# A graph network on one Trainium2 core: wider fills between gathers, 16-bit places, and one gathered tile per chunk moved to TensorE

## What is computed

```
L0  messages = h[src] * edge_weight ; summed at dst
L1  messages = silu(einsum(h[dst], edge_attr_8, W)) @ W_lin ; summed at src
L2  msg = einsum('ei,eio->eo', h[src], W_rel[edge_type]) * e ; summed at dst      (90 relations)
L3  w = kernel_net(edge_attr_6)  (a 16x16 matrix for each edge)
    four times: msg = einsum('ei,eio->eo', nodes[src], w) ; mean at dst ; gelu
```

## Time and profile before

| what | value |
|---|---|
| time, median of 3 runs | 28610.86 us (28602.41 to 28721.83) |
| the profiled execution's own time | 28730.07 us |
| its span | 28728.3 us |
| busy share of the span | PE 78%, PEld 43%, DVE 61%, ACT 49%, POOL 75% |
| granted TensorE clock, mean | 0.864 of full speed |
| DMA | 3120.14 MB, mean 109 GB/s |

### The profile page before, as it was taken

How to read it: one execution, slowest core, us unless ns; L and a number is a source line. 1 busy time by engine, 2 the same in 40 slices (tenths; PEclk the granted TensorE clock), 3 DMA queues, 4 the chain that set the end, 5 groups by cost and what they waited for, 6 DMA issues and landing times. The chain is left out here.

```text
span 28728.3 us, 413713 instructions
## 1 busy us (share of the span) xinstructions
PE 22502.9 (78%) x109882; PEld 12362.4 (43%) x109882; DVE 17590.5 (61%) x29340; ACT 14192.2 (49%) x24676; POOL 21497.8 (75%) x31473
## 2 busy tenths in 40 slices
PE   7888668888878888867777777688886888778886
PEld 3444345555545555533434344333333333333333
DVE  5555468888867667744444444566665666656665
ACT  6666511111135444533333333477775777667775
POOL 7888878888867667766667677677777777777777
PEclk9999879999988888877778787799898889888898
DMA  3211235555532222222222222455554555555554
GB/s 98 45 45 44 46 74 92 94 92 94 92 68 66 64 64 65 66 62 87 90 88 94 87 91 92 125 173 173 174 172 142 172 172 174 158 156 171 172 172 138
DMA packets 2201230, 3120.14 MB, mean 109 GB/s; under 512 B 782486, under 2 KB 1548644, under 8 KB 2199460
## 3 DMA queue, kind: packets, MB, share of 16 engines
q1 hardware_dynamic: 1340898, 2927.73, 31.3%
q0 software_dynamic: 790944, 162.36, 8.3%
q10 hardware_dynamic: 69282, 28.92, 0.4%
HBM read 2443.85 MB, written 673.47 MB: 109 GB/s over the span
## 5 line engine op out<-in xcount | busy, mean ns | idle before, releaser
L772 POOL DMA_INDIRECT got<-table,idx x14310 | 14075.9, 984 | 6055.7 <-issue 3081.4
L790 PE MATMUL in_place<-place_hot,tparts 128*128 128x512 fp8e4 (+1 forms) x49950 | 12106.4, 399 | 2647.8 <-ACT place_hot L995 1563.8
L995 ACT ACTIVATE place_hot<-place_b,far_lanes 128x512 fp8e4<-128x512 f32 (+1 forms) x17550 | 10586.2, 683 | 8.8 <-PE in_place L790 8.8
L790 PEld LDWEIGHTS in_place<-place_hot,tparts 128*128 128x128 bf16 x49950 | 5100.3, 105 | 9003.7 <-issue 4843.7
L1599 POOL DMA_INDIRECT added<-rows,add_idx x2160 | 3602.4, 1668 | 714.3 <-issue 654.5
L968 ACT ACTIVATE mask<-contw 128x208 f32 (+2 forms) x1350 | 555.9, 412 | 5970.6 <-DVE run L1129 2705.2
L775 POOL MEMSET rest<- 128x128 f32 (+2 forms) x14310 | 3199.8, 224 | 10.2
L1216 DVE TENSOR_TENSOR prod<-wcopy,got 128x1024 f32<-128x1024 f32 x810 | 991.5, 1227 | 2990.9 <-ACT wcopy L947 1895.6
L1642 PE MATMUL acc<-hot,spread 128*128 128x392 bf16 x12960 | 2545.4, 350 | 0.0
L1107 DVE SCALAR_TENSOR_TENSOR picked<-range_b,range_col,in_place 128x512 f32<-128x512 f16 (+1 forms) x1350 | 962.7, 713 | 2553.8 <-DMA added<-rows,add_idx 2404.6
L1171 DVE TENSOR_TENSOR prod<-w_in,rows_p 128x2048 f32<-128x2048 f32 x810 | 1846.8, 2280 | 444.7 <-ACT rows_p L983 283.7
(11 more groups left out here) (250 smaller groups left out, 21896.4 us busy)
## 6 DMA issues: line engine op xcount, KB each, us to landing
w_in<-kept SPq DMA_DIRECT2D x2430, 512.0 KB
kept<-wcopy SPq DMA_DIRECT2D x810, 512.0 KB
place_b<-place_row SPq DMA_DIRECT2D x1080, 256.0 KB
got<-table,idx POOLq DMA_INDIRECT x14310
attr<-in_edge_attr SPq DMA_DIRECT2D x270, 768.0 KB
range_b<-range_row SPq DMA_DIRECT2D x1080, 128.0 KB
rows<-in_src_row SPq DMA_DIRECT2D x270, 512.0 KB
sums<-outb SPq DMA_DIRECT2D x1350, 96.0 KB
```

Of the source, the lines that this page charges most:

```text
L772: pool.indirect_dma_start(out=got[:, r, j * W:(j + 1) * W], out_offset=None, in_=table, in_offset=bass.IndirectOffsetOnAxis(ap=idx[:, r, j ...
L790: mm = pe.matmul(in_place[b][:, h, :], tparts[:, s, t, :], place_hot[:, b, t, h * XC:(h + 1) * XC], start=(t == 0 and s == 0), stop=(t == ...
L995: ins = act.activation(place_hot[:, b, t, :], place_b[:, b, :], ACT.Abs_reciprocal_sqrt, bias=SB["far_lanes"][:, t:t + 1], scale=HOT_SLOPE ...
```

## The change

Fills are 256 columns in every pass of `edge_pass`. In the relational pass X is 4 instead of 3, so TensorE fetches four tiles of a chunk and GpSimd gathers eight instead of nine. The places are 16-bit in DRAM and in SBUF: they are stored as whole numbers, and the shift that was added to them moves into the per-partition bias of the activations (`const_far_lanes`).

```diff
+RW = 256
-        place_row = dram("place_row", (EP + 2 * CE,))
+        place_row = dram("place_row", (EP + 2 * CE,), F16)
-        range16 = sb("range16", [P, T], F16)
+        range16, place16 = sb("range16", [P, T], F16), sb("place16", [P, T], F16)
-                for row, v in ((SB["place_row"], key), (SB["range_row"], range16)):
+                for row, v in ((SB["place_row"], place16), (SB["range_row"], range16)):
-                c.step(dve.tensor_scalar(key[:, :], key[:, :], PLACE_SHIFT, None, ALU.add))
+                c.step(dve.tensor_copy(place16[:, :], key[:, :]))
-    X = {"weighted": 4, "relational": C // 4, "kernel_net": 0, "kernel_kept": 4}[kind]
+    X = {"weighted": 4, "relational": 4, "kernel_net": 0, "kernel_kept": 4}[kind]
-        rest = sb("rest", [P, {"weighted": 256, "relational": 128, "kernel_net": 32, "kernel_kept": 128}[kind] * J0])
+        rest = sb("rest", [P, J0 * RW])
-        RW = rest.shape[1] // J0
-            place_b = sb("place_b", [P, HALVES, XE])
+            place_b = sb("place_b", [P, HALVES, XE], F16)
-        "const_far_lanes": -lanes() * np.float32(HOT_SLOPE),
+        "const_far_lanes": (PLACE_SHIFT - lanes()) * np.float32(HOT_SLOPE),
```

## The result

The changed kernel takes **27,584 us** (median of 4 runs, 27,545 to 27,588) against 28,661 (4 runs, 28,602 to 28,722) for the kernel before: a ratio of 0.962, 95% interval 0.959 to 0.965, so 3.8% faster.

What follows compares the result with a forecast made beforehand. It took GpSimd to bound the weighted pass, and TensorE with its loop, slowed by holes, the relational pass. Relational -620, net -200 and kept +80 made -740, so 27,870 us; 8-in-10 range 27,600 to 29,250.

Steps and rivals of the forecast that it cites:

- The reading: Relational, net and kept passes: closely spaced GpSimd gathers go with holes in TensorE's stream, or in net long unexplained chunks.
- the tile taken from it gives nothing by itself: Relational pass: GpSimd wasn't the bound, so one gather fewer gains nothing by itself.
- the 14 that the prediction names for nine tiles: Relational pass: with nine gathered tiles and the wide fill, GpSimd would need 14 us a chunk.
- The first rival: TensorE, relational pass: holes don't come from the gathers and stay, its added work costs 675 us; 29,370 us, chance 0.27.
- Relational, -620 forecast: Relational pass: holes go, a chunk falls from 15.6 to 13.3 us, times 270 chunks is 620 us less.
- The 12.7 us of TensorE work: Relational pass: TensorE's need per chunk at full clock with four tiles, 3.9 + 8.0 + 0.8 us.
- some 0.6 of waiting for ScalarE: Relational pass: TensorE waits some 0.6 us a chunk for ScalarE's one-hot blocks, added to its 12.7 us.
- Net, -200 forecast: Net pass: gain of 200 us, taken between a gain of 367 and a loss of 635.
- The floor: Net pass: GpSimd's work with wide fills, 5075 us or 18.8 a chunk, allows a gain of at most 367 us.
- Kept, +80 forecast: Three kept passes: wider fills charged 0.1 us a chunk for uneven chunks, 80 us; bounds 0 and 252 us a pass.
- The range: Whole kernel: 27,600 to 28,200 us if the case is right, 27,600 to 29,250 for 8 in 10.
- The second rival: GpSimd becomes the bound before the gain arrives: about 28,560 us, within 0.5% of the kernel before, chance 0.13.

Runs made afterwards that it cites:

- The runs on chips 7 and 2: Chip 7: changed kernel with other fill widths or fills behind the last gather, 28,459 to 28,585 us; chip 2: five kept tiles, wide fills 26,956, narrow 28,809.
- x3_tile_only: Kernel before with only the relational pass's ninth tile moved to TensorE (four instead of three), chip 13: 28,693 us against 29,218, ratio 0.982.
- e4_places_only: Kernel before with only the places made 16-bit, chip 11: 26,340 us against 26,329, ratio 1.0004.
- e3_tile_only: Kernel before with only four instead of three relational tiles on TensorE, chip 11: 26,277 us against 26,329, ratio 0.998.
- x2_fills_only: Kernel before with only the fills made 256 columns in all passes, chip 7: 27,802 us against 29,376, ratio 0.946.
- e1_old_widths: Changed kernel with the fill widths of before (256, 128, 32, 128 columns), chip 11: 26,279 us against 26,329 for the kernel before, ratio 0.998.

## Why the prediction was right, and where it wasn't

**The reading was right.** The forecast rested on four passes in which closer gathers and holes went together, and called that a coincidence. The runs on chips 7 and 2 make it a cause, on chips that show holes at all, though not the only one. The prediction also says of the ninth tile that "the tile taken from it gives nothing by itself". That step is wrong: x3_tile_only gives 525 us, with net and kept as they were. The wide fills alone leave the relational pass at 13.9 us a chunk, the 14 that the prediction names for nine tiles. The first rival (the holes come from elsewhere: 29,370) fell. The Trainium skill's rule beside it (SBUF — State Buffer, Who interferes with whom), that a DMA never contends with a compute engine, doesn't cover what was measured: 103 waits became 855 in the weighted pass with narrower fills between the gathers, and the load of places halved.

**The sum was too small; what failed is the size of three terms.**
- *Relational, -620 forecast, -741 measured.* The 12.7 us of TensorE work were exact. The step that failed is "some 0.6 of waiting for ScalarE". It was taken over from a quick chunk with three tiles, where TensorE came to the blocks early. With four tiles TensorE has 2.2 us more of its own to do, and ScalarE only 1.4, so the wait closes: 5.9 us in the whole pass. On chip 11, without holes, it is seen by itself: 96.6 us with three tiles (e4_places_only), 1.2 with four (e3_tile_only), both with 128 columns and in the same stretch. Measured are 12.85 us a chunk, not 13.3; 0.45 x 270 is the 121 us.
- *Net, -200 forecast, -384 measured.* The floor was right (18.8 us a chunk, 367 to gain). The step that failed is taking a value between no gain and the floor, where only the closeness of the gathers was weighed and nothing spoke for a partial gain: if the spacing is the cause, the widest fill removes all holes and GpSimd's work is what is left.
- *Kept, +80 forecast, -51 measured.* The 80 were charged for uneven chunks, and the lower bound was 0. The step that failed is that charge: the passes came out a little shorter, not longer, with 24 holes for 332. The bound "nothing" excluded a gain without a reason; the spread of single chunks had grown narrower instead (8.5 to 16.9 us between the 5th and 95th percentile before, 9.9 to 13.6 after).

The three differences (121, 184, 131) with the weighted pass's 10 are 446 against the profiled executions (-1,185 for -740). The medians fell by 1,077, less than the two profiles did: the profiled execution before was slower than all its kernel's other ones, the one after the fastest of its four. The forecast also stood on a median of 28,611, which a fourth run made 28,661. So the miss of 286 us looks better than the sum was, by chance.

**The range** ended at 27,600 because it kept the relational term at its point value and kept at zero. With the relational pass at TensorE's bare 12.7 us (-780 instead of -620) its low end would have been 27,440. The 20 us that the low end also takes off are worked out from nothing in the text. The floors of three passes were all worked out there; a low end that takes them together would have held the result.

**The second rival** (GpSimd becomes the bound first) was half true: GpSimd is the bound in net and kept now, but what it costs is less than what the holes had cost. On chip 11 there are none, and it is the outcome there.

**What was not foreseen** is that the sign depends on the chip. The profile of one chip can't show it.

## What to carry to other kernels

If TensorE stands still for 0.2 to 1 us at "issue" in some passes and not in others, compare how far apart the indirect DMAs of GpSimd are issued; a filler instruction between them, not behind them, may pay, and only as wide as the engine's slack allows. When such a step removes a disturbance, take the pass's next bound as the estimate, not a point halfway, and let the range's low end be the sum of those bounds. Time such a change on several chips: here one kernel took 26,329 us on one chip and 29,376 on another, and the wide fills alone are worth 5.4% on the one with 29,376 and cost 5.7% on the other.

## What the runs showed of the hardware

- The same program took 26,329 to 29,376 us from chip to chip (11.6%), within 0.6% on each. Four numbered chips lie at 29,218 or above, one at 26,329, the first chip at 28,661. The passes with widely spaced gathers agree everywhere (weighted 12.3 to 12.4 us a chunk, scatter 15.8), those with close gathers don't (net 16.6 to 20.8, kept 11.4 to 12.7).
- In the relational pass of the kernel before the median hole is 0.46 us, and eight in ten lie between 0.24 and 0.98. What resource is disturbed isn't settled: the trace names none. TensorE isn't the only one that suffers. The 79 common standstills of net on the first chip are 76 on chip 15 with the kernel before, and none with wide fills (the changed kernel, x2_fills_only) or with narrow ones on chip 11 (e1_old_widths, e4_places_only).
- An Abs_reciprocal_sqrt of 128x512 to fp8 takes 704 ns from f16 just as from f32. The page's group for the changed kernel:

```profile
L995 ACT ACTIVATE place_hot<-place_b,far_lanes 128x512 fp8e4<-128x512 f16 x17550 | 10959.8, 704 | 12.3 <-PE in_place L790 11.3
```

- TensorE's granted clock, of full speed, is 0.87 in the relational pass of the kernel before (84% busy, with holes) and 1.00 in that of the changed one (99% busy). In net it is 0.78 with wide fills, where GpSimd is the bound, and 0.90 with narrow fills on chip 11 (11990 to 16300).
